# Attention on one core: two more of fifteen share tiles scaled by ScalarE, the order of its lines and squares changed, and the weighted sum moved inside the remainder products

## The reference

```python
attn = jnp.einsum('bhnd,bhmd->bhnm', q, k) * attn_scale
attn, a_scale = fq_act(attn)
attn = log_int_softmax(attn, a_scale)      # integer exp, then shares rounded to powers of two
out = jnp.einsum('bhnm,bhmd->bhnd', attn, v)
...
def log_int_softmax(x, sf, bits=BITS_S):
    x_int = x / sf
    x_int = x_int - x_int.max(axis=-1, keepdims=True)
    exp_int, _ = _int_exp(x_int, sf)       # 2^(n-qf) times a polynomial of the remainder r
    exp_sum = exp_int.sum(axis=-1, keepdims=True)
    ratio = jnp.where(exp_int > 0.0, exp_sum / jnp.maximum(exp_int, 1.0), BIG)
    rounds = round_ln(jnp.maximum(jnp.round(ratio), 1.0))
    ...
    return jnp.where(mask, 0.0, 2.0 ** (-qlog))
```

## Time and profile before

| | us |
|---|---|
| three runs | 1007.03, 1011.87, 1013.02 (median 1011.87) |
| the profiled execution, its own time | 1008.3 |
| its span, first to last instruction | 1006.5 |
| mean granted TensorE clock | 0.845 of full speed |
| busy of the span: VectorE, TensorE, ScalarE, GpSimd | 868.4, 703.7, 702.9, 168.8 |
| attention steps: first share instruction, last | 361.3, 733.9 |

### The profile page before, as it was taken

How to read it: one execution, slowest core, us unless ns; L and a number is a source line. 1 busy time by engine, 2 the same in 40 slices (tenths; PEclk the granted TensorE clock), 3 DMA queues, 4 the chain that set the end, 5 groups by cost and what they waited for, 6 DMA issues and landing times. The chain is left out here.

```text
span 1006.5 us, 23532 instructions
## 1 busy us (share of the span) xinstructions
PE 703.7 (70%) x6531; PEld 474.0 (47%) x6532; DVE 868.4 (86%) x2391; ACT 702.9 (70%) x1374; POOL 168.8 (17%) x276
## 2 busy tenths in 40 slices
PE   3873387747877467777777666667635486999997
PEld 3652144425555333333344333333323255999996
DVE  5898997988888899999999999999978874666676
ACT  0245365977888789999899999999844494454553
POOL 5861320017565100000000000000005430000000
PEclk9996598988999787777777877777857597999999
DMA  8000000001111111111111111111021004455552
GB/s 263 3 2 1 0 1 1 1 1 39 37 37 37 40 30 24 25 24 24 24 28 26 25 25 25 25 25 24 13 106 66 18 1 161 159 201 180 179 190 83
DMA packets 84274, 54.75 MB, mean 54 GB/s; under 512 B 53704, under 2 KB 83176, under 8 KB 83976
## 3 DMA queue, kind: packets, MB, share of 16 engines
q1 hardware_dynamic: 83208, 54.11, 17.7%
q0 software_dynamic: 1024, 0.13, 0.2%
HBM read 11.90 MB, written 3.76 MB: 16 GB/s over the span
## 5 line engine op out<-in xcount | busy, mean ns | idle before, releaser
L1159 PE MATMUL at_rem<-word,ident_half 128*128 128x459 f16 x160 | 72.6, 453 | 106.6 <-ACT expo L1286 105.1
L1383 DVE SCALAR_TENSOR_TENSOR expo<-expo,con,pow 128x153 f32<-128x153 f32 x480 | 146.1, 375 | 0.7 <-ACT expo L1286 0.7
L1286 ACT ACTIVATE expo<-at_rem,con 128x459 f32<-128x459 f32 x160 | 99.1, 641 | 7.1 <-PE at_rem L1160 4.7
L962 DVE TENSOR_REDUCE rs_ends<-rs_banks 128x770 f32 (+1 forms) x96 | 89.0, 957 | 13.6 <-PE rs_banks L934 11.3
L1242 ACT ACTIVATE pT_all<-at_pT 128x768 bf16<-128x768 int16 (+3 forms) x160 | 78.6, 558 | 18.6 <-PE at_pT L1174 13.3
L883 ACT ACTIVATE rs_banks<-rs_banks 128x770 f32<-128x770 f32 x96 | 74.1, 796 | 23.7 <-PE rs_banks L926 22.9
L1159 PEld LDWEIGHTS at_rem<-word,ident_half 128*128 128x128 f16 x160 | 15.9, 100 | 157.0 <-ACT expo L1286 151.6
L1419 DVE CUSTOM_DVE_ANT_0 weight_top<-weight_top,line 128x2448 uint16<-128x2448 uint16 x64 | 84.2, 1347 | 1.7 <-ACT line L1278 1.3
L1249 ACT ACTIVATE word<-at_banks 128x459 uint8<-128x459 f32 x160 | 82.3, 572 | 1.5 <-DVEq L1347 1.2
L1949 ACT ACTIVATE qk<-e_p,b1s 128x153 f32<-128x153 f32 x192 | 58.8, 391 | 28.4 <-PE e_p L1910 27.1
L1278 ACT ACTIVATE line<-weight_top 128x1224 f32<-128x1224 f32 x64 | 73.9, 1156 | 6.1 <-DVE weight_top L1409 6.1
(11 more groups left out here) (389 smaller groups left out, 2035.7 us busy)
## 6 DMA issues: line engine op xcount, KB each, us to landing
qk<-vt SPq DMA_DIRECT2D x64, 384.0 KB, 3.1
rs_kb<-qk SPq DMA_DIRECT2D x128, 28.7 KB, 1.9
kb<-qk SPq DMA_DIRECT2D x128, 28.7 KB, 1.9
patches<-in_patches SPq DMA_DIRECT2D x4, 768.0 KB
vi<-vt SPq DMA_DIRECT2D x32, 96.0 KB, 2.0
out<-vi SPq DMA_DIRECT2D x32, 96.0 KB, 1.9
pj_w<-in_w SPq DMA_DIRECT2D x1, 2304.0 KB, 8.4
qb<-qk SPq DMA_DIRECT2D x128, 6.0 KB, 1.8
```

The source lines that it names most:

```text
L962: v.tensor_reduce(ends[:, :, n, 5 * b:5 * b + 5], banks[:, slot(u, b), :, 0:5 * W].rearrange("p i (t n) -> p i t n", n=W), AX, ALU.max).th ...
L1159: pe.matmul(out, identh[:, :], bank(word, b).bitcast(F16), start=True, stop=False)
L1286: act.activation(bank(ex, b), rem[:, (u + b) % 2, 0:3 * N], ACT.Square, scale=2.0 ** 24, bias=c(5)).then_inc(sq_done, 1)
L1383: ins = v.scalar_tensor_tensor(ex[:, t, :], ex[:, t, :], c(7), pw[:, t, :].bitcast(BF16), ALU.add, ALU.mult, accum_out=tot[:, t:t + 1])
```

## The change

Three things are rewritten. ScalarE scales six share tiles (9 to 14) instead of four, and VectorE the other nine (0 to 8) in one instruction instead of eleven in two. The halves are divided there: half 0 is now tiles 9 to 14, which ScalarE itself has written, and half 1 tiles 0 to 8. ScalarE computes both lines one after the other and then squares banks 0, 1 and 2. On TensorE the weighted sum is taken one step earlier in the program's order: `weighted(last)` stands between remainder banks 1 and 2, instead of `weighted(gone)` after scores 4 of the next step. The transposes' first group now waits for both halves' integer adds.

```diff
-    HALF, OWN = 8, H - 1
+    OWN = H - 3
-        halves = (slice(0, HALF), slice(HALF, RT))
+        halves = (slice(OWN, RT), slice(0, OWN))
...
                 def turn(n, u, which):
                     for g in which:
-                        pe.wait_ge(i_done, n * 2 + min(g, 1) + 1)
+                        pe.wait_ge(i_done, n * 2 + 2)
...
                 def body(i, kk):
-                    now, last, gone, nxt = batch(i, kk, 0), batch(i, kk, 2), batch(i, kk, 3), batch(i, kk, -1)
+                    now, last, nxt = batch(i, kk, 0), batch(i, kk, 2), batch(i, kk, -1)
                     if now is not None:
                         n, u, half = now
                         scores(n, u, half, range(3, NB))
-                    if gone is not None:
-                        weighted(*gone)
...
                     if now is not None:
-                        remainder(n, u, range(NB))
+                        remainder(n, u, range(2))
+                    if last is not None:
+                        weighted(*last)
+                    if now is not None:
+                        remainder(n, u, range(2, NB))
...
                 steps(pe, body)
-                weighted(B - 1, 1, B // 2 - 1)
...
                 def line_of(n, h):
-                    act.wait_ge(w_done, n * 2 + h + 1)
-                    if h == 1:
+                    if h == 0:
                         act.wait_ge(a_done, n + 1)
+                    else:
+                        act.wait_ge(w_done, n + 1)
...
                 def squares(n, u, which):
                     if not first(n, 1):
-                        act.wait_ge(w_done, n * 2 - (1 if which[0] == 0 else 0))
+                        act.wait_ge(w_done, n)
...
                     for h in range(2):
                         if mid is not None:
                             line_of(mid[0], h)
-                        if now is not None:
-                            squares(now[0], now[1], ((0,), (1, 2))[h])
+                    if now is not None:
+                        squares(now[0], now[1], range(3))
...
-                        for h, half in enumerate(halves):
-                            heads = slice(half.start, min(half.stop, OWN))
-                            share = inv[:, heads].unsqueeze(2).to_broadcast([P, heads.stop - heads.start, N])
-                            v.tensor_tensor(top[:, heads, :], ex[:, heads, :], share, ALU.mult).then_inc(w_done, 1)
+                        share = inv[:, 0:OWN].unsqueeze(2).to_broadcast([P, OWN, N])
+                        v.tensor_tensor(top[:, 0:OWN, :], ex[:, 0:OWN, :], share, ALU.mult).then_inc(w_done, 1)
```

## The result

The change makes the kernel slower by 0.84%: six runs after have a median of 1018.02 us (1016.31 to 1021.32), six runs before one of 1010.14, and the ratio is 1.0084 with a 95% interval of 1.0064 to 1.0103. The profiled execution took 1017.64 us against 1008.3 before.

What follows compares the result with a forecast made beforehand. VectorE was taken as the bound, 99.5% busy at 12.0 us a step. 0.6 x 11.99 + 0.4 x 12.5 = 12.2 us; +0.2 x 31 = +6 us on 1008.3 gave 1014.5, taken as 1016 us, range 1002 to 1026.

Steps and rivals of the forecast that it cites:

- The bound and its change: Attention step: VectorE's work falls from 12.0 to 11.62 us, ScalarE's rises from 11.0 to 11.62; their chain decides.
- The step: Attention step on ScalarE: 12.2 us forecast against 12.0 before; 12.1 to 12.3 had chance 0.35.
- The kinds of step: Attention steps by TensorE's clock at remainder bank 2: high 11.99 us, low 12.38, taken as 12.5 for 0.4 of the time.
- The sum made from it: Whole kernel: +0.2 us a step over 31 attention steps, +6 us, 1014.5 on the profiled execution.
- Costs nothing: TensorE's transposes waiting for both integer adds: claimed free, as the adds are done 2 us ahead.
- The new wait: ScalarE ahead of square 2, for TensorE's remainder bank 2: 0.28 us at the high clock, 0.67 at the low.
- the prediction's signs: Profile after: ScalarE waits 0.2 to 0.6 us ahead of a square in nearly every step, never ahead of a line.
- The weighted sum: TensorE between remainder banks 1 and 2: the moved sum costs nothing, done by 3.5 us, with 1.3 us of cover.
- VectorE's loop: From ScalarE's line 1 over VectorE's nine-tile add and reciprocal to ScalarE's next shares: 11.7 us, with 0.06 for the signal.
- The saving did not carry: Rival that the attention step falls to 11.7 us, -9 us, 1000 to 1002 us; chance 0.1.
- The clock did not stay high: Rival that TensorE's low clock stays away from the attention steps: 11.99 us each, 1008 to 1012 us; chance 0.25.
- The slower rival: Remainder bank 2 at low clock in most steps, third transposes late: 12.5 to 12.7 us, 1024 to 1032 us; chance 0.25.

## Why the prediction came out right

**The bound and its change.** The prediction said that VectorE and ScalarE would be level in work at 11.62 us and the chain between them decide. ScalarE's work measured 11.62, VectorE's 0.960 x 12.21 = 11.72. VectorE's single share instruction takes 1.587 us where 1.60 was worked out from two other sizes, and six tiles on ScalarE 1.98 as laid out.

**The step.** Forecast 12.2 us, measured 12.21. The kinds of step behind it fit less well, so the agreement to 0.01 us is in part luck. Measured from one first share of ScalarE to the next between 470 and 730 us, without the last one, eleven steps with bank 2 at the high clock take 12.08 us on average, where 11.99 was laid out, and ten with it at the low clock 12.36, where the sum had 12.5; and they are half of the steps, not 0.4. The stretch up to square 2 came as laid out, 5.49 and 5.86 us against 5.50 and 5.89. From square 2 to the next share it took 6.56 us at the high clock and 6.49 at the low one, against 6.49: the extra 0.1 us that the sum gave to slow steps, for a late third group of transposes, did not show there.

The sum made from it, +6 us, was 3 us short of the profiled execution's 9.3: 7.2 us come from the steps, and 1.5 from the transposes' wait for both adds in the last batch, which I had not costed. "Costs nothing" holds inside the loop, where they are done long before, but not for the last batch. The median of 1018.02 against the forecast 1016 is a smaller difference than that between single runs (1016.31 to 1021.32). That less than 1% can hardly be told from no change was too cautious: with six runs each the interval of the 0.84% is 0.2 points wide on either side.

**The new wait.** Laid out start to start as 0.28 us at the high clock and 0.67 at the low one; the gaps in the trace are 0.20 and 0.57, and each also loses the 0.1 us by which ScalarE's instructions otherwise overlap. It came in 19 of some 19.7 steps, and none came ahead of a line, as the prediction's signs had it. That it costs time was shown by leaving out one product.

**The weighted sum.** Said to be hidden with 1.3 us of cover; TensorE waits 1.67 us behind it. That it takes the transposes' waits out of ScalarE's loop was shown in both directions, by the move alone and by moving it back; the waits of `collect` for the sum, which go with it, were not in the prediction.

**VectorE's loop.** Laid out at 11.7 us. Its signal from line to add is 0.18, not 0.06, so it stands at about 11.8, still below 12.2.

**The rivals.** The saving did not carry: 11.62 us of work on each side was no step length, because neither engine works without waits for the other. The clock did not stay high where it mattered: the mean granted clock in the windows rose from 0.78 to 0.82 up to 0.82 to 0.84, yet bank 2 came at the low clock in 11 of 22 steps, against 7 of 21. The slower rival, the low clock at bank 2 in most steps together with late third transposes, did not come either: half of the steps were low, and their mean was 12.36 and not 12.5 to 12.7. What was weaker than its tone was the picture of one wait at one bank: in the experiment with the earlier distance the waits came at three places in the row of banks, and nothing was gained.

**The rule on the engines.** "ScalarE: Activation LUTs", section "Rules for kernel authors", in the Trainium skill puts multiplications on VectorE. The runs agree for this case: a tile more on ScalarE costs 0.25 to 0.35 us a step once its loop sets the step, and saves VectorE 0.16.

## What to carry to other kernels

When one engine is at 99% and the next at 92%, the slack of the second is made of waits; before work is moved onto it, lay out its loop and ask which waits would stay and which cover each instruction gave to another's answer. Regrouping instructions that ping-pong with another engine over two buffers takes the cover away even if the work is the same. And test a change with three parts one part at a time: here the part that looked like a mere adjustment (the moved sum) is the one that pays, 0.5 us a step once ScalarE sets the step, and the part that moves load is the one that costs.

## What the runs showed of the hardware

A signal from ScalarE to VectorE ahead of the integer add took 0.18 us from the end of one to the start of the other (566.59 to 566.77, in the kernel with the square between the lines; in the kernel after 574.30 to 574.48), three times the 0.06 from a square's end to TensorE's matmul (568.97 to 569.03). VectorE's instruction there is a custom one with its wait in a separate instruction ahead; which of the two makes the difference was not tried.

Which clock TensorE has at remainder bank 2 does not follow from the idle stretch just ahead. In the kernel before, 459 columns took 0.37 us (2.4 GHz) behind 2.27 us of idling and 0.57 (1.2 GHz) behind 2.66. But behind 2.94 us of idling it took 0.56 at 484.59 us of the same trace, and 0.37 at 581.04.
